# A one-column memset behind GpSimd's last indirect DMA in a GNN and mixture-of-experts kernel

## The reference, cut to what matters

```python
deg = max((adj != 0).sum(-1), 1.0)                    # 2048 nodes
x = x + relu((a_norm @ ln(x) + ln(x)) @ W + b)        # graph layer, D = 256
xf = ln(x)
logits = xf @ gate_w.T                                # 8 experts, the best one per token
h = silu(xf @ w1[e].T) * (xf @ w3[e].T)               # I = 1024
y = (h * comb) @ w2[e].T + gelu(xf @ sw1.T) @ sw2.T
out = x + y
```

## Time and profile before

| | us |
|---|---|
| median of 3 runs | 483.42 |
| lowest and highest of them | 483.39, 485.46 |
| the profiled execution's own time | 486.0 |
| its span, first to last instruction | 484.4 |

### The profile page before, as it was taken

One profiled execution on the slowest core, in us unless ns is written; L12 is line 12 of the kernel. 1 busy time (PEld: TensorE's weight loads), 2 busy tenths in 40 slices (PEclk: granted clock), 3 DMA queues, 4 the chain that ended last, 5 costly groups with the idle time before them and its releaser, 6 DMA issues.

```text
span 484.4 us, 8954 instructions
## 1 busy us (share of the span) xinstructions
PE 445.1 (92%) x2620; PEld 380.8 (79%) x2621; DVE 270.8 (56%) x549; ACT 203.3 (42%) x449; POOL 336.5 (69%) x309
## 2 busy tenths in 40 slices
PE   5899967999989999979988999999999999999992
PEld 5788845898869878868966888888888888888872
DVE  4998687654974498767773334233433333343330
ACT  3656458464545554574542233222323322232330
POOL 2888947276985799757796467976788579884112
PEclk9999999999999999999998999999999999999998
DMA  7565442201360055568676599997999563644000
GB/s 243 192 210 172 130 129 89 100 1 47 128 216 2 1 167 182 160 217 319 179 225 187 194 393 343 326 339 248 317 326 335 166 244 87 81 61 64 0 1 0
DMA packets 41004, 82.61 MB, mean 171 GB/s; under 512 B 5008, under 2 KB 16656, under 8 KB 38928
## 3 DMA queue, kind: packets, MB, share of 16 engines
q1 hardware_dynamic: 28416, 47.60, 30.1%
q0 software_dynamic: 7536, 29.39, 19.4%
q10 hardware_dynamic: 5024, 5.27, 3.7%
HBM read 74.74 MB, written 8.41 MB: 172 GB/s over the span
## 4 chain that ended last, share of the span: by engine, by line
PE 45%; POOL 19%; issue 9%; DMA 5%; DVE 3%; ACT 3%; SPq 2%; POOLq 1%; ACTq 0%
PE bank L1356 19%; POOL a_lo L447 10%; PE bank L1383 7%; POOL ering L493 5%; PE bank L1275 4%; PE bank L1297 4%; PE bank L1384 4%; DMA ering<-in_experts 3%; PE bank L1369 3%; POOL sorted_x L522 2%; PE bank L1299 2%; DMA eraw<-in_experts 2%; POOL gel_lo L463 2%; SPq L378 1%; ACT a_hi L605 1%
## 5 line engine op out<-in xcount | busy, mean ns | idle before, releaser
L1356 PE MATMUL bank<-ering,xsT_hi 128*128 x368 | 121.6, 402 | 1.9 <-POOL ering L493 1.8
L447 POOL TENSOR_TENSOR a_lo<-araw,a_hi 128x512 fp32r<-128x512 f32 x64 | 97.0, 1533 | 27.7 <-ACT a_hi L605 27.6
L1181 PE MATMUL bank<-zz,a_hi 128*128 128x512 f32 (+1 forms) x256 | 93.0, 402 | 9.8 <-POOL a_lo L447 9.6
L1100 DVE SCALAR_TENSOR_TENSOR hid<-bank,xs,sil 128x512 f32<-128x512 f32 x46 | 34.5, 751 | 92.5 <-ACT sil L740 90.5
L1356 PEld LDWEIGHTS bank<-ering,xsT_hi 128*128 128x128 f32 x368 | 69.9, 190 | 17.5 <-issue 2.7
L493 POOL TENSOR_TENSOR ering<-eraw,ering 128x512 fp32r<-128x512 f32 x40 | 51.9, 1317 | 29.7 <-DMA ering<-in_experts 20.1
L1356 PE MATMUL bank<-ering,xsT_lo 128*128 x184 | 72.4, 393 | 0.0
L1183 PE MATMUL bank<-zz,a_lo 128*128 128x256 f32 (+1 forms) x256 | 71.7, 280 | 0.0
L740 ACT ACTIVATE sil<-bank 128x512 f32<-128x512 f32 x46 | 27.5, 598 | 101.4 <-PE bank L1356 99.3
L1383 PE MATMUL bank<-ering,hidT_hi 128*128 x184 | 67.4, 406 | 1.2 <-DVE hidT_lo L1108 1.2
L1181 PEld LDWEIGHTS bank<-zz,a_hi 128*128 128x128 f32 x256 | 48.0, 188 | 24.2 <-issue 11.7
(11 more groups left out here) (156 smaller groups left out, 826.7 us busy)
## 6 DMA issues: line engine op xcount, KB each, us to landing
araw<-in_adj_t SPq DMA_DIRECT2D x32, 512.0 KB, 3.9
eraw<-in_experts SPq DMA_DIRECT2D x48, 256.0 KB, 5.0
ering<-in_experts POOLq DMA_DIRECT2D x8, 1536.0 KB, 9.0
eraw_more<-in_experts SPq DMA_DIRECT2D x48, 256.0 KB, 5.9
ering<-in_experts POOLq DMA_DIRECT2D x8, 1024.0 KB, 6.7
ering<-in_experts POOLq DMA_DIRECT2D x8, 512.0 KB, 4.8
xs<-sorted_x ACTq DMA_DIRECT2D x20, 129.0 KB, 4.7
resid<-in_x SPq DMA_DIRECT2D x4, 512.0 KB, 9.2
```

The lines of the kernel that those rows point to most:

```text
L447: pool.tensor_tensor(a_lo[:, u % AR, :], araw[:, u // CJ, u % CJ, :], a_hi[:, u % AR, :].bitcast(F32), ALU.subtract).then_inc(adj_lo_ok, 1)
L1181: pe.matmul(acc(q, it)[:, :], a_hi[:, s, it * P:(it + 1) * P], zt, start=first, stop=False)
L1356: ins = pe.matmul(bank[2 * w + h][:, :], a[:, k, :], ering[:, bass.ds(slot, 1), part, at:at + BANK].rearrange("p a n -> p (a n)"), start=n ...
```

## The change

A tile of one float per partition, `last_word`, is placed between `std` and `deg`. One instruction is added behind the loop that issues the 23 indirect DMAs: GpSimd sets that tile to zero. The instruction waits for no semaphore and raises none, and nobody reads the tile.

```diff
@@ -108,6 +108,7 @@
     mv = place("mv", [P, QT, 2], F32)
     rstd = place("rstd", [P, QT], F32)
     std = place("std", [P, QT], F32)
+    last_word = place("last_word", [P, 1], F32)
     deg = place("deg", [P, QT], F32)
     dinv2 = place("dinv2", [P, QT], F32)
     logit = place("logit", [P, NT, E], F32)
@@ -570,6 +571,7 @@
                 pool.indirect_dma_start(out=out, out_offset=bass.IndirectOffsetOnAxis(ap=row_token[:, s:s + 1], axis=0),
                                         in_=y_rows[:, s, :], in_offset=None, bounds_check=NT * P - 1,
                                         oob_is_err=False, compute_op=ALU.add).then_inc(out_stored, 16)
+            pool.memset(last_word[:], 0.0)
```

## The result

The change made the kernel slower: median 488.31 us in 7 runs (486.68 to 489.72) against 484.97 us in 7 runs (483.39 to 485.61); the ratio is 1.0057, with a 95% interval of 1.0031 to 1.0083, that is 1.5 to 4.0 us more. (The ratio is the one on record for all runs; the two medians by themselves stand at 1.007.) The forecast was 483.5 us and no difference. The profiled execution took 487.57 us, with a span of 486.0 us; its span is 1.6 us longer than the one before.

A forecast was written before the change was run, and what follows sets the result against it. TensorE holds 45% of the chain, and GpSimd's DRAIN alone the last 3.9 us. Work before 477 us 0, memset 0.1 and shift 0 gave +0.1 us on 483.42: 483.5 us, range 479.2 to 485.0.

The forecast's parts named there:

- the tile: Tile shift: `deg` and all that follows move by 32 bytes; cost put at 0, since transposes at odd starts kept their speed.
- sign of being wrong ahead of 476 us: Before the tail: the prediction is wrong if anything ahead of 476 us moves by more than 2 us.
- Rival C: Expert ring: the shift slows landing of its loads by 10%, 2.4 us more, time 485.8 us; chance 0.04.
- The memset: Between GpSimd's last DMA and its DRAIN: costs 0.10 us, within bounds of 0 and 1.05 us.
- Rival B: Before the final DRAIN: the memset starts cold and delays it by 2.4 us or more; 485.9 us at 2.5; chance 0.04.
- The DRAIN: GpSimd's end: 5.23 us beyond the last DMA, 0.083 us for each of 63 DMAs; a memset in front removes none.
- Rival A: GpSimd's end: a memset after the last DMA leaves a short DRAIN, 3.9 us less, time 479.5 us; chance 0.30.
- The sum: Whole kernel: 0 before 477 us, 0.1 memset, 0 shift, so +0.1 us on the median 483.42, giving 483.5 us.

## Why the prediction was wrong

*The step that failed* is the tile: "I cost the shift at 0". It rested on transposes whose minimum and median didn't vary though the starts of their inputs differ by 8 bytes each. But minimum and median of a duration don't show the distance between starts, and those transposes are not the kind of matmul that the loop is made of, which stream 512 columns of the ring against weights from another tile. The move costs 4.4 ns in each of 552 matmuls, 2.4 us in all, where I had put 0. The ratio of the change, 1.5 to 4.0 us, and that of the tile alone, 0.7 to 2.7 us, both hold it. The forecast's sign of being wrong ahead of 476 us, a move by 2 us, was not met by the profiled pair (1.45 us), in which the fall of the clock inside the loop before hid 1.6 us.

*Rival C* had the sign, the carrier (the ring) and the place in the profile (VectorE's last addition later, tail unchanged), with a chance of 0.04. It named later landing of loads as the mechanism; the runs show the matmuls. The one longer wait for split weights, ahead of the seventh step, comes and goes from run to run at unchanged distances. I had argued against it with the same rows 11. Its price of 2.4 us was a threshold, not a measurement, and agrees with the 2.4 us here by chance.

*The memset* was right: 0.11 us behind the DMA for the 0.10 forecast, and the whole with the tile elsewhere is 0.9999. Rival B didn't come: this trace shows 0.11 us, for an instruction whose kind had last run over 470 us before. The Trainium skill gives about 6 us for the first call to freshly loaded code (GPSIMD Engine Reference, Instruction dispatch, on wrapper-ucode dispatch). No such cost shows here; whether any code was loaded for this memset no row shows, so the figure itself isn't tested.

*The DRAIN* was right too. Rival A, with 0.30, is out: behind a memset it is as long as behind the DMA. The estimate of 0.083 us for each DMA since the last DRAIN was made from one DRAIN; 0.083 for 61 and 0.084 for 40 bear it out, and 0.094 for 23 is 13% above it.

*The sum* was compared with a median of three runs, 483.42 us, that lay at the low end of what the kernel does: over 29 to 35 runs its median was 485.6 to 486.0 us. Against those, even "no difference" would have ended above the range's end of 485.0. The ratio, not the level, is what shows that the change is slower.

## What to carry to other kernels

A tile that nobody reads can cost time through where it puts the others: compare the distance between starts of the bounding matmuls, not their durations, and try a pad before concluding that an instruction is to blame. Where GpSimd has issued many DMAs, look at how long the DRAIN at the end of its program lasts beyond the last of them. Here it grew with the number issued since the DRAIN before, and an explicit DRAIN in an earlier gap of its work took 0.8% off this kernel, while a memset as its last instruction took nothing off.

## What the runs showed of the hardware

- The up matmuls, which stream 512 float32r columns, start 231 to 238 ns apart, depending on the distance, within 256 bytes, between the starts of the weight tile and of the streamed tile in SBUF: 0 is best, 64 is 2 ns worse, 96 to 192 are 5 to 7 ns worse. That distance is shown as the cause by moving either tile alone and by moving both together. Why it counts stays open, and so does whether the pattern repeats every 256 bytes; distances of 32, 160 and 224 weren't tried.
- The down matmuls, whose weights and ring kept the distance 0 in the change and in most of the runs, were still 183.1 to 186.3 ns apart (mean of their two kinds) without a pattern that these runs explain; that is up to 1.2 us over 368 matmuls. The three pads before the ring moved their distance too, to 32, 128 and 192, and gave 183.5, 184.8 and 186.2 ns, all inside that range. So the finding on the up matmuls isn't shown for other matmuls.
- GpSimd's DRAIN takes 0.083 to 0.094 us for each DMA that GpSimd has issued since its last DRAIN, counted from the end of the last instruction before it: 5.23 us for 63, 5.06 for 61, 3.36 for 40, 2.16 for 23. For 2 it ends with the landing, 1.30 us. A memset between the DMAs and the DRAIN doesn't shorten it.
